# Four graph layers on one core: layer norms' small steps joined in pairs, one statistics instruction for two graphs, the message summed in one bank, heads split on GpSimd, turned probabilities copied by VectorE

## What is computed

```
h = relu(layernorm(x)); x = x + L0(h)   # attention over neighbours, 128 wide, and its features beside it
h = relu(layernorm(x)); x = x + L1(h)   # deg * (h Wi + b) + adj @ (h Wj)
h = relu(layernorm(x)); x = x + L2(h)   # 8-head masked attention, output projection
h = relu(layernorm(x)); x = x + L3(h)   # attention over neighbours, 256 wide
```

## Time and profile before

| | |
|---|---|
| median of 3 runs | 1142.57 us |
| span of the profiled execution, first to last instruction | 1144.0 us |
| instructions | 38802 |
| TensorE matmuls, busy | 1054.0 us, 92% |
| ScalarE, busy | 1056.3 us, 92% |
| VectorE, busy | 1043.0 us, 91% |
| GpSimd, busy | 949.6 us, 83% |
| mean granted TensorE clock | 0.987 |
| DMA: bytes, mean rate | 190.05 MB, 166 GB/s |

### The profile page before, as it was taken

One profiled execution on the slowest core, in us unless ns is written; L12 is line 12 of the kernel. 1 busy time (PEld: TensorE's weight loads), 2 busy tenths in 40 slices (PEclk: granted clock), 3 DMA queues, 4 the chain that ended last, 5 costly groups with the idle time before them and its releaser, 6 DMA issues.

```text
span 1144.0 us, 38802 instructions
## 1 busy us (share of the span) xinstructions
PE 1054.0 (92%) x14872; PEld 883.0 (77%) x14872; DVE 1043.0 (91%) x2911; ACT 1056.3 (92%) x3145; POOL 949.6 (83%) x1734
## 2 busy tenths in 40 slices
PE   4689999999999999999999999999999999999964
PEld 3467888788878878887887888888888888888752
DVE  4489999999999999999999999999999999999961
ACT  3489999999999999999999999999999999999862
POOL 3888899889989989988898988889888988998521
PEclk9899999999999999999999999999999999999997
DMA  5369999999999999999999999999999999999872
GB/s 149 68 110 167 180 177 182 167 187 171 181 176 178 171 169 182 180 179 168 182 167 179 183 178 173 169 189 171 174 176 183 170 168 190 180 174 156 151 139 51
DMA packets 643514, 190.05 MB, mean 166 GB/s; under 512 B 607232, under 2 KB 643328, under 8 KB 643328
## 3 DMA queue, kind: packets, MB, share of 16 engines
q1 hardware_dynamic: 642560, 187.24, 94.9%
q10 hardware_dynamic: 768, 0.33, 0.1%
HBM read 19.73 MB, written 16.78 MB: 32 GB/s over the span
## 4 chain that ended last, share of the span: by engine, by line
ACT 47%; DMA 16%; POOL 14%; PE 12%; DVE 9%; issue 3%; POOLq 0%; SPq 0%; DVEq 0%
DMA h_t<-h_rows 11%; PE ps L403 3%; DMA mix_t<-mix_rows 3%; PE ps L405 3%; PE ps L404 3%; ACT ps L1053 3%; ACT ps L1042 3%; ACT ps L1048 3%; ACT ps L1059 3%; POOL h_rows L1189 3%; POOL h_rows L1249 2%; ACT relu L973 2%; ACT relu L964 2%; ACT query_hi L1030 2%; ACT key_hi L1033 2%
## 5 line engine op out<-in xcount | busy, mean ns | idle before, releaser
L403 PE MATMUL ps<-w_hi,h_t 128*128 128x256 f16 (+2 forms) x1280 | 330.5, 265 | 31.4 <-DMA h_t<-h_rows 28.3
L404 PE MATMUL ps<-w_lo,h_t 128*128 128x256 f16 (+2 forms) x1280 | 329.5, 264 | 0.0
L405 PE MATMUL ps<-w_hi,h_t 128*128 128x256 f16 (+2 forms) x1280 | 326.4, 264 | 0.0
L403 PEld LDWEIGHTS ps<-w_hi,h_t 128*128 128x128 f16 x1280 | 125.3, 98 | 53.7 <-DMA h_t<-h_rows 33.0
L403 PE MATMUL ps<-h_t,w_hi 128*128 128x256 f16 x512 | 139.6, 273 | 0.0
L405 PE MATMUL ps<-h_t,w_lo 128*128 128x256 f16 x512 | 139.6, 273 | 0.0
L404 PE MATMUL ps<-h_t,w_hi 128*128 128x256 f16 x512 | 139.6, 273 | 0.0
L405 PEld LDWEIGHTS ps<-w_hi,h_t 128*128 128x128 f16 x1280 | 125.6, 98 | 14.3
L404 PEld LDWEIGHTS ps<-w_lo,h_t 128*128 128x128 f16 x1280 | 126.3, 99 | 13.2
L1185 POOL TENSOR_SCALAR h_rows<-relu 128x512 f16<-128x512 f32 x64 | 39.5, 618 | 64.3 <-ACT relu L964 64.3
L403 PEld LDWEIGHTS ps<-v_hi,head_t_hi 128*128 128x128 f16 x1024 | 79.9, 96 | 8.8 <-issue 2.3
(11 more groups left out here) (181 smaller groups left out, 4622.4 us busy)
## 6 DMA issues: line engine op xcount, KB each, us to landing
x<-in_x SPq DMA_DIRECT2D x64, 256.0 KB, 3.9
out<-x SPq DMA_DIRECT2D x64, 256.0 KB, 2.7
h_t<-h_rows SPq DMA_TRANSPOSE x256, 3.6
head_t_hi<-head_hi SPq DMA_TRANSPOSE x64, 4.7
head_t_lo<-head_lo SPq DMA_TRANSPOSE x64, 6.2
mix_t<-mix_rows SPq DMA_TRANSPOSE x64, 3.4
w_f<-in_w_o SPq DMA_DIRECT2D x1, 256.0 KB, 4.1
w3t_f<-in_w_t SPq DMA_DIRECT2D x1, 256.0 KB, 3.8
```

Of the source, the lines that this page charges most:

```text
L403: pe.matmul(o, lh, rh, start=start, stop=False)
L404: pe.matmul(o, lh, rl, start=False, stop=False)
L405: return pe.matmul(o, ll, rh, start=False, stop=stop)
```

## The change

**Joined small steps.** The statistics of layers 0 and 2 now stand in one tile `stats02` and those of 1 and 3 in `stats13`, each [128, 2, 2, 3]. The small steps run on 128x4 for two layers at once: chain `02` for layer 0 of group g and layer 2 of group g - 3, chain `13` for layer 1 of g and layer 3 of g - 5. The first step of a chain waits for both statistics. Chain `13` has a fifth step, `scale_rstd13`.

**Joint statistics.** One `bn_stats` reads both graphs of a group alternately (one element of the first, one of the second, 1 KB apart), so its two halves, which count even and odd elements, are the two graphs. The `bn_aggr` go; epsilon's step divides by D.

**Message in one bank.** The degree is multiplied into layer 1's normaliser, the messages are divided by it, and the adjacency carries the weights' scale. So `message_own` and `gather` accumulate in one bank, and one `update1` remains, which now waits for `add_deg_bias` too.

**Heads.** `head_norm` writes fp32 to SBUF (`mix_f`). GpSimd splits both graphs at once (`rows_hi_mix`, `rows_lo_mix`); ScalarE's `keep_out` and VectorE's `split_out` go.

**Turned probabilities.** `keep_probs0` and `keep_probs3` are VectorE `tensor_copy` instructions.

**Order.** All banks are dealt anew, the waits for them with them, and every engine's `slot` is written in another order. `PARTS` is 9 for 7.

```diff
-        mj_ps = ps[1]
-        mi_ps = ps[4]
-        ag_ps = ps[3]
+        mj_ps = ps[2]
+        mi_ps = ps[6]
...
             def message_own(g):
...
-                        last = triple(mi_ps[:, b * D:(b + 1) * D], ...
-                                      start=(c == 0), stop=(c == KC - 1))
-                last.then_inc(message_own_done, 1)
+                        triple(mi_ps[:, b * D:(b + 1) * D], ...
+                                      start=(b == 0 and c == 0), stop=False)
             def gather(g):
                 pe.wait_ge(split_message_done, g + 1)
-                pe.matmul(ag_ps[:, :], agg[:, :], mj_hi[g % 2][:, :], start=True, stop=False)
-                last = pe.matmul(ag_ps[:, :], agg[:, :], mj_lo[g % 2][:, :], start=False, stop=True)
-                last.then_inc(gather_done, 1)
+                pe.matmul(mi_ps[:, :], agg[:, :], mj_hi[g % 2][:, :], start=False, stop=False)
+                pe.matmul(mi_ps[:, :], agg[:, :], mj_lo[g % 2][:, :], start=False, stop=True).then_inc(gather_done, 1)
...
-                dve.bn_stats(stats2[g % 2][:, 0, :], x[g % XBUF][:, 0, :])
-                dve.bn_stats(stats2[g % 2][:, 1, :], x[g % XBUF][:, 1, :]).then_inc(stats2_1_done, 1)
-                dve.wait_ge(stats2_1_done, g + 1)
-                dve.bn_aggr(moments2[g % 2][:, 0, :], stats2[g % 2][:, 0, :])
-                dve.bn_aggr(moments2[g % 2][:, 1, :], stats2[g % 2][:, 1, :]).then_inc(mean_var2_done, 1)
+                dve.bn_stats(stats02[(g + 3) % 2][:, 1, :, :].rearrange("p b s -> p (b s)"), x[g % XBUF][:, :, :].rearrange("p b d -> p d b")).then_inc(both_stats2_done, 1)
...
-                dve.wait_ge(gather_done, g + 1)
-                dve.wait_ge(update1_own_done, g + 1)
-                dve.tensor_tensor(x[g % XBUF][:, :, :], ag_ps[:, :]..., x[g % XBUF][:, :, :], ALU.add).then_inc(update1_done, 1)
+                dve.wait_ge(add_deg_bias_done, g + 1)
+                dve.wait_ge(gather_done, g + 1)
+                dve.scalar_tensor_tensor(x[g % XBUF][:, :, :], mi_ps[:, :]..., degree_unscale[:, 0:1], x[g % XBUF][:, :, :], ALU.mult, ALU.add).then_inc(update1_done, 1)
...
-                act.activation(mj_hi[g % 2][:, :], mj_ps[:, :], ACT.Copy, scale=UNSCALE).then_inc(keep_message_done, 1)
+                act.activation(mj_hi[g % 2][:, :], mj_ps[:, :], ACT.Copy, scale=message_unscale[:, 0:1]).then_inc(keep_message_done, 1)
...
+            def keep_probs0(g):
+                dve.wait_ge(turn_probs0_0_done, g + 1)
+                dve.tensor_copy(prob_t0[g % 2][:, :], p0_ps[:, 0:GROUP * P]).then_inc(keep_probs0_done, 1)
...
+            def add_eps13(g):
+                if g < graph_groups:
+                    pool.wait_ge(both_stats1_done, g + 1)
+                if g >= 5:
+                    pool.wait_ge(both_stats3_done, g - 4)
+                pool.tensor_scalar(vareps13[g % 2][:, :, :], stats13[g % 2][:, :, :, 2], 1.0 / D, EPS, ALU.mult, ALU.add).then_inc(add_eps13_done, 1)
+            def power13(g):
+                pool.wait_ge(add_eps13_done, g + 1)
+                pool.tensor_tensor(rstd13[g % 2][:, :, :], vareps13[g % 2][:, :, :], minus_half[:, :, :], ALU.pow).then_inc(power13_done, 1)
...
+            def rows_hi_mix(g):
+                pool.wait_ge(head_norm_1_done, g + 1)
+                pool.tensor_scalar(mix_rows[g % 2][:, 0, :, :], mix_f[g % 2][:, :, :], 1.0, 0.0, ALU.mult, ALU.add).then_inc(rows_hi_mix_done, 1)
+            def rows_lo_mix(g):
+                pool.wait_ge(rows_hi_mix_done, g + 1)
+                pool.tensor_tensor(mix_rows[g % 2][:, 1, :, :], mix_f[g % 2][:, :, :], mix_rows[g % 2][:, 0, :, :], ALU.subtract).then_inc(rows_lo_mix_done, 1)
```

More of the change, by code:

```diff
@@ L21 @@
 BANK = 512
-FOLD = [0, 1, 2, 5]
+FOLD = [0, 1, 2, 4]
 EPS = 1e-5
@@ L32 @@
 XBUF = 11
-PARTS = 7
+PARTS = 9
 COL_W3 = 0
@@ L292, in build, with at @@
         expo3_1_done = sem("expo3_1_done")
+        turn_probs3_0_done = sem("turn_probs3_0_done")
+        keep_probs3_done = sem("keep_probs3_done")
         inv_sum3_done = sem("inv_sum3_done")
-        turn_probs3_1_done = sem("turn_probs3_1_done")
-        keep_probs3_done = sem("keep_probs3_done")
         gat_sum3_done = sem("gat_sum3_done")
-        update3_0_done = sem("update3_0_done")
+        update3_1_done = sem("update3_1_done")
         def run(slot):
             for t in range(graph_groups + PARTS):
-                def at(part, piece):
-                    if 0 <= t - part < graph_groups:
+                def at(part, piece, more=0):
+                    if 0 <= t - part < graph_groups + more:
                         piece(t - part)
@@ L394, in _ @@
         def _(pe):
-            def turn(bank, src, b):
-                for c in range(KC):
-                    last = pe.transpose(bank[:, (c * GROUP + b) * P:(c * GROUP + b + 1) * P], src[:, b, c * P:(c + 1) * P], ident[:, :])
-                return last
             def triple(o, lh, ll, rh, rl, start, stop):
@@ L667, in link, with setup_w0 @@
                 dve.wait_ge(vector_setup, done)
-            dve.memset(minus_half[:, :], -0.5).then_inc(norm_consts, 1)
+            for k in range(2):
+                dve.memset(stats02[k][:, :, :, :], 1.0)
+            for k in range(2):
+                dve.memset(stats13[k][:, :, :, :], 1.0)
+            dve.memset(minus_half[:, :, :], -0.5).then_inc(norm_consts, 1)
+            dve.wait_ge(norm_consts, 1)
+            def setup_w0():
+                dve.wait_ge(w0_folded, 1)
+                dve.tensor_copy(w0_f[:, :, F0:F0W], ps[FOLD[0]][:, 0:2 * KC].rearrange("p (c k) -> p c k", c=KC)).then_inc(w0_ready, 1)
             def setup():
@@ new lines, in slot @@
+                at(8, both_stats3)
+                at(6, head_max_3)
+                at(3, inv_sum0)
+                at(3, update0_1)
+                at(3, update0_0)
+                at(3, both_stats1)
+                at(6, head_max_2)
+                at(9, keep_probs3)
+                at(4, split_message)
+                at(9, inv_sum3)
+                at(6, head_max_0)
+                at(9, update3_0)
+                at(6, split_head_3)
+                at(7, invert_heads_0)
+                at(9, update3_1)
@@ L947, in _ @@
+                at(7, head_norm_0)
+                at(7, invert_heads_1)
+                at(7, head_norm_1)
+                at(6, head_max_1)
+                at(1, both_stats0)
+                at(4, update1)
+                at(6, split_head_0)
             run(slot)
@@ new lines, in expo3_1 @@
+                act.activation(prob3[g % 2][:, 1, :], leaky3[g % 2][:, 1, :], ACT.Exp, bias=nmax3[g % 2][:, 1:2], accum_out=sum3[g % 2][:, 1:2]).then_inc(expo3_1_done, 1)
+            def slot(at):
+                at(7, keep_head_1)
+                at(6, cast_key)
+                at(3, expo0_1)
+                at(6, cast_query)
+                at(3, expo0_0)
+                at(7, keep_value)
+                at(9, keep_feat3_0)
+                at(9, keep_feat3_1)
+                at(2, norm0_0)
+                at(2, norm0_1)
+                at(9, leaky3_1)
+                at(9, leaky3_0)
+                at(5, norm2_1)
+                at(5, norm2_0)
+                at(9, expo3_1)
+                at(9, expo3_0)
+                at(6, head_exp_3)
+                at(4, keep_message)
+                at(6, keep_head_3)
+                at(6, head_exp_2)
+                at(8, norm3_1)
+                at(8, norm3_0)
+                at(6, head_exp_0)
+                at(3, norm1_0)
+                at(3, norm1_1)
+                at(2, keep_feat0)
+                at(6, keep_head_2)
+                at(6, keep_head_0)
+                at(6, head_exp_1)
+                at(2, leaky0_1)
+                at(2, leaky0_0)
```

643 lines of the change are left out of this document (249 added, 394 removed).

## The result

The changed kernel takes 1171.68 us (median of 4 runs, 1168.57 to 1174.77); beside it the kernel before took 1142.30. The ratio is 1.0243, 95% interval 1.0222 to 1.0264: slower, where the prediction said 1117 us. The profiled execution took 1174.77 us, 3.1 above that median, with a span of 1173.0.

The account below looks back on a forecast made before the run. ScalarE bounds before (16.4 of 16.60 us a period), GpSimd after: 16.1 plus 0.1 makes 16.2. 63 x 0.40 = 25.2 off the 1144.0 us span gives 1118.8, less 1.4: 1117 us; own range 1109 to 1127, with rivals 1098 to 1140.

Parts of the forecast that it names:

- I cost it at nothing: SyncE's queue: move1 is ready late behind move_out, store and load, and message_source waits; hidden, so 0 us.
- I leave filling and draining as they are: Start and end of the run: shorter chains and longer powers about cancel, pipeline about as deep; no change.
- so I take 0.1: Waits of the bounding engine, GpSimd: 0.1 us a period on top of 16.1, giving 16.2; ScalarE lost 0.25 before.
- GpSimd's 16.1: GpSimd's need in us per period after the change, up from 15.5, with each power growing by 0.51.
- its 0.78 us in the period shown: TensorE's idle time in one 16.76 us period before the change, subtracted to get its need of 15.8 to 16.0.
- the 25.2 us that the forecast saved: Gaps between groups: 63 times the period's fall from 16.60 to 16.20 us.
- The other needs: Us per period on the engines besides GpSimd: TensorE 15.8 to 16.0, ScalarE 15.4, VectorE 14.7.
- the two ends: GpSimd's power of four elements: no growth from 0.704 us, or 0.51 more each; the upper end was taken.
- Rival 1: GpSimd's power doesn't grow: it needs 15.1, TensorE bounds, period 16.0, 1105 us; chance 0.22.
- Rival 2: GpSimd's order: waits for ScalarE's norm add 0.3 to 0.5 us a period, about 1136 us; chance 0.18.
- Rival 3: VectorE's joint bn_stats at half pace, 1.20 us each: period 17.2, about 1181 us; chance 0.08.
- The prediction's last test: TensorE waiting over 0.3 us a period for move1 or the split message while GpSimd idles would disprove the forecast's cause.

Follow-up runs that it names:

- e1: Changed kernel with SyncE's store and load ahead of layer 3's transfer instead of behind that of the projected heads; 1157.8 us.
- e5: Changed kernel with ScalarE's one-time first-group work on two weights moved behind both halves of layer 0's first normaliser; 1163.9 us.
- e3: Changed kernel with the powers in both joint chains replaced by products, so the scales are not the reference's; 1151.8 us.
- e6: Changed kernel with both the edit of e1 (store and load first) and that of e5 (one-time work later); 1149.1 us.
- e13: Kernel e6 with SyncE's load ahead of the store instead of behind it; 1140.7 us.
- e7: Kernel e6 with each store writing only 8 of its group's 128 rows; 1141.5 us.
- e8: Kernel e5 with store and load issued from ScalarE's queue, so SyncE issues transposes alone; 1150.9 us.

## Why the prediction was wrong

The forecast of the span, 1118.8 us, was 54.2 too low: 40.5 in the gaps between groups (1048.9 against 1033.6 - 25.2 = 1008.4) and 13.8 in filling and draining.

**The step that failed.** "SyncE: move_out, the store, the load and move1 stand behind each other now ... I cost it at nothing, hidden behind message_source of the group before". The place was right, the price was not. It was 0.3 us a period: e1 changes nothing else and takes 17.3 us out of the gaps. Part of that is the clock, which fell behind two such waits (last section). Two details were off. The wait landed not at message_source, which move1 still reaches, but at head_sum behind it, whose transposes stand further back in the same queue. And I priced one wait by whether its own data were late, not the whole run of issues by where it ends: the rows of SyncE show 13 us of 16.6 taken in one piece.

**The second step that failed.** "I leave filling and draining as they are". 6.1 us of filling is the one-time work between two halves of a norm; e5 gives back 6.8 in the first column and 7.8 in all. I had read the order of the steady part only. Of the 7.7 us of draining the power's latency is a part (e3: 4.2 less without it, though its 0.8 is more than the 0.3 that the change added to each power); the rest was not separated. The mean granted clock while draining is 0.75 in the changed kernel and was 0.84; whether that is a cause or follows from more waiting isn't shown.

**The third: "so I take 0.1".** The sum was the largest need of one engine, 16.1, plus 0.1 for its waits. The need was right. Measured as the prediction measures it, as a period less its idle time (median of the periods between 120 and 1040 us), GpSimd needs 16.08 in the changed kernel and 16.07 in e6. The waits were not: 41.5 us of them in these 920, 0.8 us a period, and 0.47 in e6, where both mended causes are gone and the period is still 16.55. The longest, first in the changed kernel:

```profile
POOL h_rows L1105 <- ACT relu L911: 17.0, 26, 1.5
POOL mix_rows L1167 <- DVE mix_f L820: 14.2, 20, 2.0
```

TensorE's own account says where they come from. It waited 26.8 us in the same 920 in the kernel before, nearly all for transposes; 33.5 in the changed kernel, 23.8 in e6 and 16.9 in e13. Its need stayed at 16.0 to 16.2. The prediction subtracted its 0.78 us in the period shown and never added any back, as if such waits would go once ScalarE was relieved. They stayed, and with two engines that need 16.1 nothing is left to hide them. So most of the 25.2 us that the forecast saved could not be had without the transposes landing in time.

**Right by luck.** GpSimd's 16.1 is the sum of two errors that cancel. The new chains take 3.56 us from start to start, not the 3.80 charged with the power at 1.21; the old ones took 4.9, not 5.16, because neighbouring steps overlap.

**The other needs**, by the same measure in e6: TensorE 16.1 (forecast 15.8 to 16.0), ScalarE 15.7 (15.4), VectorE 15.4 (14.7). The relief of VectorE was 0.7 smaller than my sum had it, which I didn't break down. The base was a little off too: 16.60 was read from one stretch, and the mean of the middle 53 gaps is 16.56, 2.5 us in 63.

**What was right.** The durations: bn_stats at 0.7, copies at 0.4, the merged update like the one before; that ScalarE stops being the fullest engine; and that GpSimd becomes a bound. The power, taken at 1.21, is 1.03: between the two ends, 0.16 us for each further element.

**The rivals.** Rival 1: the power grew, by 0.32 of 0.51. Rival 2 comes nearest in its mechanism: with 16.1 to do, each wait of GpSimd comes on top. Its price was 0.3 to 0.5 us a period; the changed kernel has 0.8, e6 0.47. What it has wrong is the place: GpSimd's order doesn't make the waits, late transposes do. Rival 3, by its time (1181) the closest, is refuted in its cause: the joint bn_stats takes 0.705 us for 512 elements where 256 took 0.42. The Trainium skill's rule behind it (Advanced Engine Details and Errata, SBUF Cachelines: a new line with each access pays a penalty) doesn't show here; the measurement decides. The prediction's last test, TensorE waiting for a transpose while GpSimd has idle time, is what came, only behind the heads' transfer: 24.8 us.

**Open.** What makes single transposes land late in some periods and not in others: fewer bytes (e7) and an earlier load (e13) both lessen it, an own queue for store and load (e8) doesn't, and no run removes it. Whether a kernel with both GpSimd and TensorE relieved would be faster. And most of the longer draining.

## What to carry to other kernels

Where one queue issues most transfers in order, write out its issues over a period with ready, issued and needed times before costing a change of order at nothing; send what nobody awaits (a load far ahead) where the queue is idle, not ahead of what an engine will want. When relieving an engine gives nothing, look for a second one that is as long, and look in undisturbed periods at which engine has no wait at all. Don't go by the busy share for that: GpSimd was full at 93 to 94% busy, since the pauses between dependent small steps count as neither busy nor idle. Count waits for transfers as a cost of their own; relieving the fullest engine doesn't take them away. And read the first group's path by itself, since one-time work hangs on pieces whose order the change turns round.
